# Key-value products on four column tiles, row sums of four batches in one product, and a rewritten order of steps, in a three-block transformer layer on one core

## The chip, the cores and the metric

The kernel runs on one core of one Trainium2 chip. The metric is the time of one execution on the device in microseconds (us); less is better. In the profile PE is TensorE (PEld its weight loads), DVE VectorE, ACT ScalarE, POOL GpSimd and SP SyncE, which issues most transfers.

## What is computed

The input x is 8 batches of 64 tokens with 256 features; ctx_1024 is 8 batches of 1601 rows with 256 features. Three blocks follow each other, each on a layer norm of the sum so far:

```python
x = x + xattn(layernorm(x), ctx, ctx, mask)   # 16 heads of 16, no softmax: (Q K^T / dk) V
x = x + attn(layernorm(x))                    # 16 heads, causal softmax over 64 tokens
x = x + ffn(layernorm(x))                     # rotary attention, rmsnorm, gated dense layer and 8 experts, rmsnorm
```

Since the first block has no softmax, Q (K^T V) is computed: from a batch's rows one needs the Gram matrix of ctx (256 x 256) and the sums of its rows. K^T V is kept only where row and column belong to the same head of 16 features.

## The kernel before

One program writes out the instructions of all engines. `steps_in_order` (L173) joins four tables of steps (L87 to L171), and each engine walks through the same list and issues what it has to do for a step. So the list sets the order on every engine at once; what an engine does for a step then waits on semaphores.

The 512 tokens are four tiles of 128 (two batches each), in two halves. The steps and the lines that matter here:

- `gram` n multiplies chunk n of ctx (24 chunks, three to a batch) with itself on TensorE. Before it, `split` n cuts the chunk into a high part (ScalarE) and a low part (VectorE, L1134). `evac` b copies a batch's Gram matrix out.
- `cross1` to `cross4` b make the first block of batch b. `cross1` transposes parts of the Gram matrix; `cross2_product` (L791) multiplies it with the value weights and, for odd b, multiplies the row sums of batches b-1 and b with these weights (4 products with 2 columns); `cross3` (L812) multiplies with the key weights, 4 products of 128 x 128, from which VectorE keeps the heads (L1174); `cross4` (L824) multiplies with the queries. For odd b VectorE then adds the part of the row sums (L1181) to tile b/2.
- A tile goes through `xo_product`, `turn_z`, `proj1_product`, `score_product` (L868), `turn_p`, `values`, `project` (L905), and the same again for the rotary attention (second index 1), then `square` on ScalarE, `rms1` on VectorE and GpSimd, `rms1_end` on VectorE, and `turn_x` (L938): a transpose on TensorE, a copy `xHL` on ScalarE, a subtraction on VectorE (L1261), a copy `xT` on ScalarE.
- `hidden_product`, `shared_product` and `experts_product` are the dense layers, 0 to 7 of the hidden layer for the first half, 8 to 15 for the second. They need few small steps and stand between the steps of the tiles. `hidden_product` 0 and 8 wait for the subtraction of `turn_x` of both tiles of their half.
- `norm0` i is the first layer norm of half i; on VectorE its statistics wait for the transfer of x (L1100).

All matmuls go through one helper (L698), all transposes through another (L701). A product of plain f32 operands shows as two instructions in the trace, one of the rounded type as one. The part of the code for key-value products and for the causal bars:

```python
for ob in range(KC):
    for k in range(KC):
        last = mm(ps[:, CROSS_B[0], D + ob * P:D + (ob + 1) * P], w0[:, 1, k, ob * P:(ob + 1) * P],
                  cv[:, k, ob * P:(ob + 1) * P], k == 0, k == KC - 1)
```

Of the kernel before, what the change touches and what calls it, by code (L numbers as in the profile page):

```python
# [86 lines left out]
def opening_steps():  # L87

    return [
        ("gram", 0), ("split", 0), ("gram", 1), ("split", 1), ("split", 2), ("gram", 2), ("split", 3), ("split", 4),  # L90
        ("evac", 0), ("gram", 3), ("cross1", 0), ("split", 5), ("norm0", 0), ("gram", 4), ("cross2_product", 0),
        ("gram", 5), ("norm0_end", 0), ("cross2", 0), ("split", 6), ("pre", 0), ("cross3", 0), ("evac", 1),
        ("split", 7), ("split", 8), ("q0_product", 0), ("gram", 6), ("cross4", 0), ("qb", 0), ("flag", 0),
        ("cross1", 1), ("norm0", 1), ("gram", 7), ("split", 9), ("cross2_product", 1), ("norm0_end", 1),
        ("cross2", 1), ("split", 10), ("gram", 8), ("pre", 1), ("cross3", 1), ("split", 11), ("evac", 2),
        ("q0_product", 1), ("cross4", 1), ("cross1", 2), ("gram", 9), ("qb", 1), ("flags", 0),
    ]

# [1251 lines left out]
```

## Time and profile before

| | |
|---|---|
| Median of 3 runs | 244.86 us (244.59 to 245.79) |
| The profiled execution | 244.46 us |
| Its span in the trace | 242.6 us |
| TensorE busy | 233.2 us, 96% |
| VectorE / ScalarE / GpSimd busy | 170.6 / 123.3 / 79.1 us |
| Bytes moved | 26.34 MB, 109 GB/s on average |

The span lies inside the execution's own time, 1.9 us less. The profile gives for each engine how long it was busy, for groups of instructions how long one takes, and in a timeline when each began and what ended the idle time before it. Matmuls are pipelined: the next one starts before the last one's record ends, so the distance from start to start is what one costs.

### The profile page before, as it was taken

Reading aid. Unit: us, or ns where it says so; the run is one execution under the profiler, and the core shown is the slowest. Engines: PE = TensorE matmul, PEld = TensorE weight load, DVE = VectorE, ACT = ScalarE, POOL = GpSimd, SP = SyncE. Lnnn points to the kernel's source line nnn. Section 1 sums busy time; section 2 is a strip of 40 time slices with the busy share of each in tenths; the row PEclk is TensorE's granted clock in tenths of the full one; section 3 lists DMA queues with packets and bytes.
Section 4 is the critical chain, followed back from the end, with each engine's and each line's share of the span. In section 5 each row is a group of like instructions: output and inputs, shape, how many; then the busy total and the mean of one; then the engine's idle time right before and its main releaser. Section 6 shows DMA issues by size and latency. Waiting matters only on the chain.

```text
span 242.6 us, 5335 instructions
## 1 busy us (share of the span) xinstructions
PE 233.2 (96%) x2112; PEld 210.5 (87%) x2112; DVE 170.6 (70%) x370; ACT 123.3 (51%) x246; POOL 79.1 (33%) x89
## 2 busy tenths in 40 slices
PE   6989999999999999999999999999999999999992
PEld 6979999998988989788999898997878889998881
DVE  1758885785968787978873785696999755378443
ACT  3753826266356457673455897792551444540000
POOL 3011136224423040512759359725500020650101
PEclk9999999999999999999999999999999999999998
DMA  6899999765023341803033223200000000000000
GB/s 228 270 315 387 262 400 389 280 191 170 3 86 89 97 107 69 269 5 89 0 91 93 84 86 89 86 3 0 4 0 3 0 3 0 3 22 22 5 22 22
DMA packets 9433, 26.34 MB, mean 109 GB/s; under 512 B 1464, under 2 KB 2752, under 8 KB 9280
## 3 DMA queue, kind: packets, MB, share of 16 engines
q1 hardware_dynamic: 9120, 25.47, 32.3%
q10 hardware_dynamic: 288, 0.52, 0.6%
q8 instruction: 17, 0.28, 0.5%
q14 instruction: 8, 0.07, 0.1%
HBM read 25.46 MB, written 0.52 MB: 107 GB/s over the span
## 4 chain that ended last, share of the span: by engine, by line
PE 76%; issue 6%; ACT 5%; DMA 5%; DVE 3%; POOL 2%; SPq 1%; POOLq 0%; DVEq 0%; ACTq 0%
PE ps L698 71%; PE ps L701 5%; DMA w<-in_w 3%; DMA raw<-in_ctx 2%; POOL w L495 1%; ACT probT L508 1%; ACT w L508 1%; POOL rstd L460 1%; POOL hT L499 1%; ACT L682 1%; ACT L619 1%; ACT ch L572 0%; ACT prob L619 0%; DVE Z L1292 0%; DVE cl L1134 0%
## 5 line engine op out<-in xcount | busy, mean ns | idle before, releaser
L698 PE MATMUL ps<-ch 128*128 128x130 f32 (+1 forms) x208 | 51.5, 265 | 0.9 <-DVE cl L1134 0.9
L698 PE MATMUL ps<-ch,cl 128*128 128x260 f32 (+1 forms) x208 | 51.1, 308 | 0.0
L698 PE MATMUL ps<-w,hT 128*128 128x512 f32 (+1 forms) x204 | 45.8, 382 | 0.0
L698 PEld LDWEIGHTS ps<-w,hT 128*128 128x128 f32 x204 | 36.4, 188 | 7.4 <-issue 0.3
L460 POOL TENSOR_TENSOR rstd<-ve,half_exp 128x1 f32<-128x1 f32 (+1 forms) x22 | 15.9, 723 | 82.5 <-DVE ve L1013 82.4
L1134 DVE TENSOR_TENSOR cl<-raw,ch 128x1024 fp32r<-128x1024 f32 (+4 forms) x31 | 32.7, 1069 | 11.9 <-ACT ch L572 11.6
L698 PEld LDWEIGHTS ps<-ch 128*128 128x128 f32 (+1 forms) x208 | 39.5, 190 | 1.7 <-ACT ch L572 1.0
L698 PEld LDWEIGHTS ps<-ch,cl 128*128 128x128 f32 (+1 forms) x208 | 39.2, 188 | 0.2
L572 ACT ACTIVATE ch<-raw 128x1024 fp32r<-128x1024 f32 (+4 forms) x31 | 27.7, 917 | 9.7 <-DMA raw<-in_ctx 8.6
L698 PE MATMUL ps<-xHL,dense 128*128 128x256 f32 x192 | 25.0, 287 | 0.0
L698 PEld LDWEIGHTS ps<-xHL,dense 128*128 128x128 f32 x192 | 23.6, 191 | 0.3
L495 POOL TENSOR_TENSOR w<-raw,w 128x1024 fp32r<-128x1024 f32 x8 | 18.9, 2374 | 10.1 <-ACT w L508 10.1
L1292 DVE SCALAR_TENSOR_TENSOR Z<-ps,w,Z 128x256 f32<-128x256 f32 x32 | 15.4, 482 | 7.6 <-PE ps L698 6.8
L499 POOL TENSOR_TENSOR hT<-sa,hT 128x256 fp32r<-128x256 f32 x16 | 12.7, 812 | 15.7 <-ACT hT L508 15.7
L698 PE MATMUL ps<-w,gs 128*128 128x256 f32 x64 | 15.5, 385 | 0.8 <-DMA w<-in_w 0.8
L477 POOL TENSOR_TENSOR gpre<-gab 128x130 f32<-128x130 f32 x16 | 8.4, 545 | 22.1 <-ACT gab L508 22.1
L527 ACT ACTIVATE sq<-Z 128x256 f32<-128x256 f32 x8 | 3.3, 414 | 22.8 <-DVE Z L1292 19.2
L508 ACT ACTIVATE probT<-ps 128x512 f32<-128x512 f32 x16 | 8.6, 600 | 11.0 <-PE ps L701 11.0
L698 PEld LDWEIGHTS ps<-w,gs 128*128 128x128 f32 x64 | 11.5, 189 | 2.8 <-issue 1.3
L495 POOL TENSOR_TENSOR dense<-stage,dense 128x1024 fp32r<-128x1024 f32 x4 | 9.4, 2369 | 12.6 <-ACT dense L508 12.6
L1211 DVE TENSOR_REDUCE mx<-ps 128x16 f32<-128x1024 f32 x8 | 9.8, 1221 | 4.9 <-PE ps L698 4.9
L619 ACT ACTIVATE prob<-prob 128x1024 f32<-128x1024 f32 x8 | 8.5, 1057 | 8.9 <-DVE prob L1212 8.9
(160 smaller groups left out, 429.8 us busy)
## 6 DMA issues: line engine op xcount, KB each, us to landing
raw<-in_ctx SPq DMA_DIRECT2D x22, 512.0 KB, 4.5
raw<-in_w SPq DMA_DIRECT2D x8, 512.0 KB, 3.6
stage<-in_dense SPq DMA_DIRECT2D x4, 512.0 KB, 7.2
w<-in_w SPq DMA_DIRECT2D x4, 256.0 KB, 6.1
w<-in_w SPq DMA_DIRECT2D x1, 1024.0 KB, 7.4
mask<-in_mask SPq DMA_DIRECT2D x1, 800.5 KB, 6.7
raw<-in_ctx SPq DMA_DIRECT2D x8, 65.0 KB
raw<-in_ctx ACTq DMA_DIRECT2D x2, 256.0 KB, 4.7
```

The lines of the kernel that those rows point to most:

```text
L460: pool.tensor_tensor(rstd[:, lo:hi], ve[:, lo:hi], half_exp[:, lo:hi], ALU.pow).then_inc(sem("rstd"), 1)
L477: last = pool.tensor_tensor(gpre[:, i % 2, k, :], gab[:, i % 2, k, k, :], gab[:, i % 2, k, k + 1, :], ALU.add)
L495: pool.tensor_tensor(piece(i, 1), raw_piece(i), f32(piece(i, 0)), ALU.subtract).then_inc(sem("piece_low"), 1)
L499: pool.tensor_tensor(hT[:, m // 4, 1, m % 4, :], sa[:, m % 4, :], f32(hT[:, m // 4, 0, m % 4, :]), ALU.subtract).then_inc(sem("h_low"), 1)
L508: act.activation(dst, src, ACT.Copy).then_inc(signal, 1)
L572: act.activation(halves(ch[:, c, lo:n, :])[:, :, :, 0:P], halves(raw[:, ROWS * c + lo:ROWS * c + n, :]), ACT.Copy).then_inc(sem("high_done ...
L619: act.activation(prob[:, t % 2, :, :], prob[:, t % 2, :, :], ACT.Exp, scale=SCALE).then_inc(own("prob", t), 1)
L698: return pe.matmul(o, l, r, start=start, stop=stop, skip_group_check=not check)
L701: return pe.transpose(o, src, ident)
L1134: dve.tensor_tensor(halves(cl[:, c, lo:n, :]), halves(raw[:, ROWS * c + lo:ROWS * c + n, :]), halves(f32(ch[:, c, lo:n, :]))[:, :, :, 0:P] ...
L1211: link(dve.tensor_reduce(mx[:, k, :], got, AX.X, ALU.max))
L1292: ins = dve.scalar_tensor_tensor(out=Z[:, t, :], in0=ps[:, DENSE_B[bank % 4], e * D:(e + 1) * D], scalar=w8[:, t, 2 * u + e:2 * u + e + 1] ...
```

## The change

- `cross3` on TensorE now makes only the blocks of 32 x 32 on the diagonal: for each of the 4 products of before there are 4 small ones (128 rows, 32 columns of weights, 32 moving columns), whose results stand on four different groups of 32 partitions. VectorE multiplies the smaller result, repeated, with the same mask of heads.
- Row sums: `SUMS = {1: 2, 3: 2, 7: 4}`. The sums of batches 4 to 7 go through the value weights together, in step 7. So the products of step 5 are gone, and the additions for tiles 2 and 3 come after `cross4` 7. `xo_product` 2 therefore stands behind `cross4` 7.
- Causal bars in `score_product` kind 0: the two products contract over 64 rows each instead of 128, on different halves of the rows.
- The four tables of steps are rewritten. The set of steps is the same.

```diff
+SUMS = {1: 2, 3: 2, 7: 4}
+PAIR = 2 * HD
...
-        ("gram", 0), ("split", 0), ("gram", 1), ("split", 1), ("split", 2), ("gram", 2), ("split", 3), ("split", 4),
-        ("evac", 0), ("gram", 3), ("cross1", 0), ("split", 5), ("norm0", 0), ("gram", 4), ("cross2_product", 0),
+        ("gram", 0), ("gram", 1), ("split", 0), ("split", 1), ("gram", 2), ("split", 2), ("split", 3), ("split", 4),
+        ("evac", 0), ("gram", 3), ("norm0", 0), ("split", 5), ("gram", 4), ("norm0_end", 0), ("cross1", 0),
...
-                    if i % 2:
+                    if i in SUMS:
                         pe.wait_ge(sem("scol"), i + 1)
+                        n = SUMS[i]
                         for jb in range(KC):
                             for k in range(KC):
-                                last = mm(ps[:, CROSS_B[0], jb * 2:(jb + 1) * 2], w0[:, 2, k, jb * P:(jb + 1) * P],
-                                          scol[:, k, i - 1:i + 1], k == 0, k == KC - 1)
+                                last = mm(ps[:, CROSS_B[0], jb * n:(jb + 1) * n], w0[:, 2, k, jb * P:(jb + 1) * P],
+                                          scol[:, k, i + 1 - n:i + 1], k == 0, k == KC - 1)
...
                     for ob in range(KC):
                         for k in range(KC):
-                            last = mm(ps[:, CROSS_B[0], D + ob * P:D + (ob + 1) * P], w0[:, 1, k, ob * P:(ob + 1) * P],
-                                      cv[:, k, ob * P:(ob + 1) * P], k == 0, k == KC - 1)
+                            for r in range(P // PAIR):
+                                pair = slice(ob * P + r * PAIR, ob * P + (r + 1) * PAIR)
+                                last = mm(ps[r * PAIR:(r + 1) * PAIR, CROSS_B[0], D + ob * PAIR:D + (ob + 1) * PAIR],
+                                          w0[:, 1, k, pair], cv[:, k, pair], k == 0, k == KC - 1)
...
                         for g in range(2):
-                            mm(ps[:, tile_bank(t) + g, :].rearrange("p (c k) -> p c k", k=S), unit[:, :],
-                               bars[:, :].unsqueeze(1).to_broadcast([P, H // 2, S]), True, False, False)
+                            rows_ = slice(g * S, (g + 1) * S)
+                            mm(ps[:, tile_bank(t) + g, :].rearrange("p (c k) -> p c k", k=S), unit[rows_, :],
+                               bars[rows_, :].unsqueeze(1).to_broadcast([S, H // 2, S]), True, False, False)
...
-                elif step == "cross4" and i % 2:
-                    t = i // 2
-                    dve.wait_ge(sem("qsv"), t + 1)
+                elif step == "cross4" and i in SUMS:
                     dve.wait_ge(sem("ctxT"), i + 1)
-                    mine = ctxT[:, t // TH, :, (t % TH) * P:(t % TH + 1) * P]
-                    dve.tensor_tensor(mine, mine, qbT[:, :, t * P:(t + 1) * P], ALU.add).then_inc(sem("corrected"), 1)
+                    for t in range((i + 1 - SUMS[i]) // 2, (i + 1) // 2):
+                        dve.wait_ge(sem("qsv"), t + 1)
+                        mine = ctxT[:, t // TH, :, (t % TH) * P:(t % TH + 1) * P]
+                        dve.tensor_tensor(mine, mine, qbT[:, :, t * P:(t + 1) * P], ALU.add).then_inc(sem("corrected"), 1)
```

**Opening, VectorE.** `cl` is a split's low part (128x1280 is chunk 5), `gs` are the additions of `cross1` 0, `st`, `mv` and `ve` the statistics of `norm0` 0. Before:

```order
L1134 TENSOR_TENSOR cl<-raw,ch 128x512 x4
L1142 TENSOR_TENSOR gs<-gpre,ps 128x256
L1144 TENSOR_TENSOR gs<-gab,ps 128x128
L1145 TENSOR_TENSOR gs<-gab,ps 128x128
L1134 TENSOR_TENSOR cl<-raw,ch 128x1280
L1018 BN_STATS st<-X 128x6 x2
```

With the change:

```order
L1145 TENSOR_TENSOR cl<-raw,ch 128x512 x4
L1029 BN_STATS st<-X 128x6 x2
L1032 BN_AGGR mv<-st 128x2 x2
L1024 TENSOR_SCALAR ve<-mv 128x2
L1145 TENSOR_TENSOR cl<-raw,ch 128x1280
L1040 TENSOR_SCALAR Z<-X,mv,rstd 128x256 x2
L1153 TENSOR_TENSOR gs<-gpre,ps 128x256
```

The statistics of x moved ahead of chunk 5's low part, and the additions of `cross1` 0 behind both. On TensorE `gram` 4 moved ahead of `cross1` 0, and `gram` 5 and the turn of z ahead of `cross2_product` 0.

**End of the first half's attention, TensorE.** `probT,vz` is `values` (1,1), `wo,aT` its `project`, `cv,w` `cross3`, `q0T,mb` `cross4`, `cst,Z` a turn (of z or x), `w,ctxT` `xo_product`, `xHL,dense` `hidden_product`. Before:

```order
L698 MATMUL ps<-probT,vz 32x64 x32
L698 MATMUL ps<-q0T,mb 128x64 x2
L701 MATMUL ps<-cst,gab 128x128 x4
L698 MATMUL ps<-wo,aT_99 128x256 x2
L701 MATMUL ps<-cst,Z 128x128 x2
L698 MATMUL ps<-w_52,gs 128x256 x4
L698 MATMUL ps<-scol,w_52 128x2 x4
L698 MATMUL ps<-zT,w_67 128x128 x8
L698 MATMUL ps<-cv,w_52 128x128 x4
L698 MATMUL ps<-w_67,zT 128x256 x2
L698 MATMUL ps<-q0T,mb 128x64 x2
L701 MATMUL ps<-cst,Z 128x128 x2
```

With the change:

```order
L705 MATMUL ps<-probT,vz 32x64 x32
L705 MATMUL ps<-wo,aT_99 128x256 x2
L705 MATMUL ps<-cv,w_52 32x32 x16
L708 MATMUL ps<-cst,Z 128x128 x2
L705 MATMUL ps<-q0T,mb 128x64 x2
L708 MATMUL ps<-cst,Z 128x128 x2
L705 MATMUL ps<-w_52,ctxT 128x256 x2
L705 MATMUL ps<-xHL,dense 128x256 x36
```

Behind `values` (1,1) there stood `cross4` 6 and `cross1` 7 and, behind `project` (1,1), two stages of tile 2. Now `project` (1,1) follows `values` (1,1) at once, and `cross3` 7, `cross4` 7 and two turns are all that stands between it and `xo_product` 2 and `hidden_product` 0.

**End of the second half's attention, TensorE.** `cst,prob` is `turn_p`, `w,hT` with 12 instructions is one `experts_product`. Before:

```order
L698 MATMUL ps<-w_49,hT 128x512 x36
L701 MATMUL ps<-cst,prob 128x128 x16
L698 MATMUL ps<-probT,vz 32x64 x64
L698 MATMUL ps<-wo,aT_98 128x256 x2
L698 MATMUL ps<-wo,aT_99 128x256 x2
L698 MATMUL ps<-w_49,hT 128x512 x12
L701 MATMUL ps<-cst,Z 128x128 x4
L698 MATMUL ps<-w_49,hT 128x512 x12
L698 MATMUL ps<-xHL,dense 128x256 x72
```

With the change:

```order
L705 MATMUL ps<-w_49,hT 128x512 x36
L708 MATMUL ps<-cst,prob 128x128 x16
L705 MATMUL ps<-probT,vz 32x64 x64
L705 MATMUL ps<-wo,aT_98 128x256 x2
L705 MATMUL ps<-wo,aT_99 128x256 x2
L705 MATMUL ps<-w_49,hT 128x512 x12
L708 MATMUL ps<-cst,Z 128x128 x4
L705 MATMUL ps<-xHL,dense 128x256 x96
```

One `experts_product` stood between the turns of x (`cst,Z`) and `hidden_product` 8 (`xHL,dense`); now none does.

## Rows read from the trace of the kernel before

**Rows 1.** The page, part 1: busy time, share of the span, instructions.

```profile
PE 233.2 (96%) x2112; PEld 210.5 (87%) x2112; DVE 170.6 (70%) x370; ACT 123.3 (51%) x246; POOL 79.1 (33%) x89
```

**Rows 2.** Timeline of TensorE, 14 to 19 us; in brackets the idle time before.

```profile
15.02 0.63 PE L701 MATMUL ps<-cst,gab 128*128 128x128 f32 x4 [0.44 <-ACT gab L508]
...
18.32 0.89 PE L698 MATMUL ps<-w,gs 128*128 128x256 f32 x3 [0.79 <-DMA w<-in_w]
```

**Rows 3.** Waits of TensorE: us in total, times, longest.

```profile
PE ps L698 <- ACT aT L508: 0.5, 1, 0.5
```

**Rows 4.** Groups of TensorE instructions, shapes apart: busy us, mean ns | idle before.

```profile
L698 PE MATMUL ps<-w,hT 128*128 128x512 f32 x180 | 43.0, 395 | 0.0
...
L698 PE MATMUL ps<-cv,w 128*128 128x128 f32 x64 | 8.4, 275 | 0.0
...
L698 PE MATMUL ps<-probT,vz 64*32 64x64 f32 x512 | 6.9, 224 | 0.1
...
L698 PE MATMUL ps<-q0T,mb 128*128 128x64 f32 x32 | 4.6, 268 | 0.0
...
L698 PE MATMUL ps<-blank 128*128 128x128 f32 x18 | 4.1, 423 | 1.0 <-POOL blank L443 1.0
```

**Rows 5.** Timeline of TensorE, two stretches: start us, us, instruction.

```profile
32.98 0.95 PE L698 MATMUL ps<-scol,w 128*128 128x2 f32 x8
33.79 0.31 PE L698 MATMUL ps<-ch 128*128 128x130 f32 x1
...
56.83 0.70 PE L698 MATMUL ps<-bars,unit 128*128 128x512 f32 x2
57.46 1.16 PE L698 MATMUL ps<-kblk,qp 64*128 64x128 f32 x16
```

**Rows 6.** The transfers: issue, count, size, us from issue to landing.

```profile
X<-in_x SPq DMA_DIRECT2D x1, 512.0 KB, 6.2
```

**Rows 7.** Timeline of SyncE's queue, 10 to 24 us.

```profile
11.29 0.34 SPq L407 DMA_DIRECT2D X<-in_x  x1
```

**Rows 8.** Timeline of VectorE, 10 to 24 us.

```profile
17.64 1.49 DVE L1134 TENSOR_TENSOR cl<-raw,ch 128x1280 fp32r<-128x1280 f32 x1 [0.91 <-ACT ch L572]
19.05 0.74 DVE L1018 BATCH_NORM_STATS2 st<-X 128x6 f32<-128x256 f32 x2
...
20.11 0.17 DVE L1013 TENSOR_SCALAR ve<-mv 128x2 f32<-128x2 f32 x1
```

**Rows 9.** Timeline of all engines, 110.4 to 117.9 us.

```profile
110.76 0.38 ACT L508 ACTIVATE aT<-ps 128x256 f32<-128x256 f32 x1 [1.23 <-PE ps L698]
...
112.72 0.41 DVE L1230 TENSOR_TENSOR Z<-Z,ps 128x256 f32<-128x256 f32 x1
...
113.94 0.55 POOL L460 TENSOR_TENSOR rstd<-ve,half_exp 128x1 f32<-128x1 f32 x1 [4.88 <-DVE ve L1013]
...
114.53 0.63 DVE L1041 SCALAR_TENSOR_TENSOR Z<-Z,rstd,rows 128x256 f32<-128x256 f32 x1 [0.31 <-POOL rstd L460]
```

**Rows 10.** Groups of VectorE instructions, shapes apart.

```profile
L1090 DVE CAST topf<-topi 128x16 f32<-128x16 uint32 x2 | 2.3, 1172 | 0.1
```

**Rows 11.** Timeline of all engines, 188.6 to 200 us.

```profile
197.18 0.60 PE L701 MATMUL ps<-cst,Z 128*128 128x128 f32 x4
...
197.60 0.38 ACT L508 ACTIVATE xHL<-ps 128x256 fp32r<-128x256 f32 x1 [2.02 <-PE ps L701]
...
198.54 0.39 ACT L508 ACTIVATE xT<-ps 128x256 f32<-128x256 f32 x1 [0.56 <-DVE xHL L1261]
198.82 0.38 ACT L508 ACTIVATE xHL<-ps 128x256 fp32r<-128x256 f32 x1
199.24 0.42 DVE L1261 TENSOR_TENSOR xHL<-ps,xHL 128x256 fp32r<-128x256 f32 x1 [0.73 <-ACT xHL L508]
```

**Rows 12.** Stretches: length; busy us of PE, PEld, DVE, ACT, POOL; granted clock; DMA.

```profile
237.90:240.30 2.40, 0.00 (x0) 0.00 (x0) 1.24 (x4) 0.51 (x2) 0.66 (x1) 1.00 0.00 0
240.30:242.60 2.30, 0.00 (x0) 0.00 (x0) 0.19 (x1) 0.00 (x0) 0.00 (x0) 0.51 0.17 57
```

More of the change, by code:

```diff
@@ L124, in second_half_steps @@
-        ("rotate", 1), ("keys2", 1), ("gram", 20), ("exp", (0, 1)), ("evac", 6), ("values2", 1), ("roped", 1),
-        ("keys_roped", 1), ("cross2_product", 5), ("shares", (0, 1)), ("cross2", 5), ("split", 23),
-        ("turn_p", (0, 1)), ("score_product", (1, 1)), ("values", (0, 1)), ("score", (1, 1)), ("project", (0, 1)),
-        ("square", 0), ("rms1", 0), ("exp", (1, 1)), ("cross3", 5), ("rms1_end", 0), ("gram", 21), ("cross4", 5),
-        ("cross1", 6), ("piece", 3), ("turn_x", 0), ("piece", 4), ("shares", (1, 1)), ("gram", 22),
@@ L129, in second_half_steps @@
-        ("cross2_product", 6), ("xo_product", 2), ("cross2", 6), ("xo", 2), ("xo_end", 2), ("norm1", 2), ("gram", 23),
-        ("turn_p", (1, 1)), ("cross3", 6), ("evac", 7), ("values", (1, 1)), ("cross4", 6), ("norm1_end", 2),
-        ("cross1", 7), ("piece", 5), ("piece", 6), ("project", (1, 1)), ("turn_z", (2, 0)), ("cross2_product", 7),
-        ("cross2", 7), ("square", 1), ("proj1_product", 2), ("rms1", 1), ("cross3", 7), ("queries", 2), ("keys1", 2),
-        ("rms1_end", 1), ("values1", 2), ("cross4", 7), ("turn_x", 1), ("piece", 7), ("score_product", (2, 0)),
@@ new lines, in second_half_steps @@
+        ("score", (1, 0)), ("cross4", 4), ("cross1", 5), ("exp", (1, 0)), ("norm2_end", 0), ("shares", (1, 0)),
+        ("split", 21), ("gram", 18), ("split", 22), ("gram", 19), ("turn_z", (0, 1)), ("cross2_product", 5),
+        ("proj2_product", 0), ("cross2", 5), ("turn_p", (1, 0)), ("keys2", 0), ("rotate", 0), ("values", (1, 0)),
+        ("roped", 0), ("cross3", 5), ("keys_roped", 0), ("project", (1, 0)), ("values2", 0), ("gram", 20),
+        ("score_product", (0, 1)), ("norm2", 1), ("piece", 2), ("norm2_end", 1), ("evac", 6), ("turn_z", (1, 1)),
@@ new lines, in second_half_steps @@
+        ("turn_p", (1, 1)), ("square", 0), ("cross2_product", 7), ("rms1", 0), ("rms1_end", 0), ("piece", 6),
+        ("cross2", 7), ("values", (1, 1)), ("project", (1, 1)), ("cross3", 7), ("square", 1), ("rms1", 1),
+        ("turn_x", 0), ("rms1_end", 1), ("cross4", 7), ("turn_x", 1), ("xo_product", 2), ("hidden_product", 0),
+        ("hidden_product", 1), ("xo", 2), ("xo_end", 2), ("norm1", 2), ("norm1_end", 2), ("hidden", 0),
+        ("hidden_product", 2), ("xo_product", 3), ("turn_z", (2, 0)), ("xo", 3), ("hidden", 1), ("piece", 7),
@@ L153, in second_half_steps @@
-        ("experts_product", (1, 3)), ("last_square", 0),
+        ("project", (2, 1)), ("project", (3, 1)), ("square", 2), ("square", 3), ("rms1", 3), ("rms1", 2),
+        ("rms1_end", 3), ("rms1_end", 2), ("experts_product", (1, 3)), ("turn_x", 3), ("turn_x", 2),
     ]
```

133 lines of the change are left out of this document (72 added, 61 removed), and 3 rows, old and new, of the table USES.

## The prediction

> **What bounds the kernel now.** I read the page's first part, then TensorE's groups, then its waits, then the timeline at the places where the order changes. The page says that TensorE is busy 233.2 of 242.6 us, and no other engine over 171 [rows 1]. TensorE's waits are few: the reader is to see that the two largest of the opening lie in its timeline, 0.44 us before `cross1` 0 and 0.79 us before `cross2_product` 0 [rows 2], and that the list has one of 0.5 us for ACT's copy `aT`, between a `values` and its `project` [rows 3]. So between the first products and the last, work taken from TensorE comes off the time, and each new wait of TensorE goes on top. The other engines matter only where TensorE runs out of other work while they hand over a tile.
>
> **What is taken from TensorE.**
>
> *Key-value products.* One batch's `cross3` has 8 instructions with full weights: 8.4 us over 8 batches, 1.05 each [rows 4]. Now it has 32, each on a quarter of the columns. The nearest row is `values`, which also alternates among four column groups: 512 instructions in 8 blocks take 6.9 us, 0.86 a block of 64 [rows 4]. Both figures hold some 0.2 us in which only the last instruction drains. Half a block costs 0.33 + 0.2 = 0.53, which would save 0.52. But `values` also uses two row groups, which the new products can't. I take 0.60, a saving of 0.45, and 3.6 us over 8 batches. One end: the groups hide nothing of each other, the instructions cost a quarter of a full one's (1.05 - 0.2) / 8 = 0.106, 32 x 0.027 = 0.85, and nothing is saved. Other end: the rate of `values` and a little more, 0.55 saved, 4.4 us.
>
> A rule speaks against the small products. The Trainium skill ("TensorE: Matmul & The Clock Gate", section "Wait — 56ns, not 53.3ns?") says that matmuls never start less than about 25 ns apart, however small. By it 32 would take an estimated 0.8 us, the saving would be 0.05 to 0.1 a batch, and the time about 3 us above my sum. The trace disagrees for tiles: 64 instructions of `values` in 0.86 us are 13 ns apart with the drain counted in [rows 4].
>
> *Row sums.* A step's 8 instructions take from 32.98 to 33.79, 0.81 us, though they have two columns [rows 5]. With four columns I take the same. One step of four goes: 0.8 us. GpSimd and VectorE do the same multiplications and additions, only later.
>
> *Bars.* Two instructions from 56.83 to 57.46, 0.63 us [rows 5]. On two halves of the rows they can run together, as the pairs after them do: 16 instructions of `kblk,qp` in 1.16 us. I take half, 0.31 saved, 1.25 over four tiles; ends 0 and 1.25.
>
> Together 3.6 + 0.8 + 1.25 = 5.65 us, with ends 0.8 and 6.45. VectorE's multiplication with the heads has as many elements as before and costs nothing new.
>
> **What the order adds.**
>
> *Opening.* x is issued at 11.29 and lands 6.2 us later, at 17.5 [rows 6, 7]. Before, chunk 5's low part came first (17.64, 1.49 us), and the statistics after it, by which time x was there [rows 8]. Now VectorE stands at the statistics until 17.5, needs from 19.05 to 20.28, 1.23 us, for them, and ends chunk 5 at 17.5 + 1.25 + 1.5 = 20.25. `gram` 5 can't start before about 20.3. TensorE has less to do till then: `gram` 4 took from 15.46 (15.02 and 0.44 for four transposes, 0.63 less the drain) to the wait before 18.32, which began at 17.53 [rows 2], less the drain 1.9 us. It can now follow `gram` 3 at about 14.5, ends at 16.4, `cross1` 0 at 16.8. So TensorE idles 3.5 us, where it lost 0.44 + 0.79 and about 0.3 of restarting. The loss is 2.0 us. `cross2_product` 0 waits for the additions behind chunk 5 and fills nothing. SyncE's queue, which loads chunk 8 when chunk 5's low part is done, is later by the same microsecond, and has three chunks in hand. Nothing later gives this back, since TensorE hardly waits there. Ends: 1.0, if x lands a microsecond earlier, and 2.5.
>
> *Before `xo_product` 2.* `project` (1,1) now directly follows `values` (1,1): that is the 0.5 us of [rows 3], at 110.76 in [rows 9]. From a `project` to the turn of its x: hand-over 0.2, then from the addition at 112.72 to the end of the scaled row at 114.53 + 0.63 = 115.16 [rows 9]; 2.7 us with the hand-over to TensorE. The cover is `cross3` 7 (0.5), a turn of two transposes (0.22) and `cross4` 7 (4.6 us over 8 batches is 0.57 [rows 4]), some 1.25. 1.5 us stay open. `xo_product` 2 waits then for the additions that ACT's `ctxT` and VectorE make behind that chain, an estimated 0.4. In all 2.4 us. Queued behind VectorE's wait for the mean square are the remainder of `turn_x` 0 and these additions. GpSimd's root has `piece` 6 and two multiplications with the row sums ahead of it, which could add up to 0.5. Ends 0.5 and 3.0.
>
> *Second half, rotary part.* `project` (2,0) on VectorE stands behind `shares` (3,0) and `gate_best` 0, a string of small instructions, of which one conversion alone takes 1.17 us [rows 10]. TensorE has `values` (3,0) and one `experts_product` as cover, 0.86 + 12 x 0.24 = 3.7 us [rows 4], against 2.7 for the chain and the queue ahead. I take 1.0 us; ends 0 and 2.
>
> *Before `hidden_product` 8.* The reader is to see in [rows 11] that four transposes start at 197.18, and that the second tile's `xHL` is subtracted until 199.66; one `experts_product` covered it. Now `experts_product` (1,3) stands ahead of the turns, where it covers the roots, and nothing follows them. From 197.2 to 199.7 less 0.44 of transposes is 2.1 us of idle TensorE. Ends 1.5 and 2.5.
>
> What I cost at nothing: the rest of the first half, where `gram` chunks stand in twos and threes and tiles 0 and 1 move against them, a few tenths of waits for a few tenths; the tail, where `finish` 2 moved behind the last experts' additions, beside ACT's square (that cover is 0.6 us, about its size); the bars' copies on ACT.
>
> **Sum.** 244.46 - 5.65 + 2.0 + 2.4 + 1.0 + 2.1 = 246.3 us. It is made against the profiled execution, which lies 0.4 under the median of 244.86. A measurement of this kernel tells 0.5% (1.2 us) from no change, so the forecast is just over that line.
>
> **The rivals.**
>
> 1. *The hand-overs are covered, and it is faster.* The two places that I had to piece together from several engines' queues, before `xo_product` 2 and in the rotary part, cost nothing, and the products save their upper end: 244.46 - 0.8 - 1.25 - 4.4 + 2.0 + 2.1 = 242.1. It decides once these two places together stay below about 1 us. For it: in the old order TensorE waits at almost none of its hand-overs. Against it: the covers counted above are short. Chance 0.27.
> 2. *Savings and waits cancel.* Half of those two places: 244.6. Chance 0.15.
> 3. *The clock falls in the opening.* After its last matmul TensorE stood still from 237.9, and the granted clock was 1.00 until 240.3 and 0.51 after it [rows 12]: it fell from 2.4 to 1.2 GHz after 2.4 us of standing. The opening's new gap is 3.5 us. The start shows the price of a stretch at the lower level: its 18 instructions took 4.1 us [rows 4], 0.22 each, where four transposes of the same size take 0.60 with the drain [rows 11], 0.11 each; that loses some 2 us, so 248.2. For it: the gap is longer than that at the end; against it: matmuls surround it. Chance 0.12.
> 4. *The column groups don't run side by side*, so the change doesn't do what it says: 246.3 + 3.6 = 249.9. `values` speaks against it. The Trainium skill (same page, section "LDWEIGHTS (loading the stationary operand)") says that a weight load's time goes with its columns alone; if loads don't overlap, that is this rival. Chance 0.10.
>
> **The numbers.** My own case has 0.36, of which 0.10 falls short of the line. Slower: 0.26 + 0.12 + 0.10 = 0.48; within 0.5%: 0.15 + 0.10 = 0.25; faster: 0.27. The range is 241.7 to 248.6: it takes in the first three rivals and leaves out the fourth, 0.10, and the far ends of the first and third, 0.1 together.
>
> **What would show it.** `cv,w` as 256 instructions with 4.5 to 5 us busy instead of 8.4; `scol,w` x24; bars at 0.3 us a pair. A wait of TensorE of 3 us or more before `gram` 5 near 17 us, ended by VectorE's `cl`, at clock 1.00. Waits of 1 to 2 us before the turn of x 1, and 2 us before `hidden_product` 8, ended by `xHL`. TensorE busy around 228 us. I am wrong if `cv,w` stays near 8 us, or if `gram` 5 starts by 19, or if no wait shows between `project` (1,1) and `hidden_product` 0.

## The result, and the profile after

| | before | after |
|---|---|---|
| Median | 244.73 us (244.45 to 245.79, 4 runs) | 249.69 us (248.79 to 250.67, 4 runs) |
| Ratio | | 1.0196, 95% interval 1.0164 to 1.0228 |
| The profiled execution | 244.46 us | 248.79 us |
| Its span, mean granted clock | 242.6 us, 0.995 | 247.0 us, 0.981 |

The kernel became 5.0 us slower. I had forecast 246.3 and a range up to 248.6: the direction was right, the size was not, and the time lies outside the range. The ratios here and below leave out executions more than 1.5% above the fastest of their kernel, which are two of e1's (248.92 and 249.55 us); medians and ranges have all of them.

The page of the changed kernel, part 1, answers to [rows 1]:

```profile
PE 232.2 (94%) x2296; PEld 206.8 (84%) x2296; DVE 172.6 (70%) x368; ACT 119.4 (48%) x243; POOL 81.0 (33%) x89
```

TensorE is busy almost as long as before, though it has less to do. Its groups, shapes apart (busy us, mean ns | idle before), answer to [rows 4]:

```profile
L705 PE MATMUL ps<-cv,w 128*32 128x32 f32 x256 | 3.7, 199 | 1.9 <-DVE svn L1178 1.9
...
L705 PE MATMUL ps<-bars,unit 64*128 64x512 f32 x8 | 2.0, 494 | 0.0
...
L705 PE MATMUL ps<-scol,w 128*128 128x2 f32 x16 | 1.9, 241 | 0.0
...
L705 PE MATMUL ps<-scol,w 128*128 128x4 f32 x8 | 1.0, 242 | 0.0
```

Key-value products take 3.7 us instead of 8.4, and one step of row sums is gone. Something else has grown. TensorE's waits (us in total, times, longest) answer to [rows 3]:

```profile
PE ps L705 <- DVE cl L1145: 4.2, 3, 3.0
PE ps L705 <- DVE svn L1178: 1.9, 1, 1.9
PE ps L705 <- DVE xHL L1276: 1.7, 1, 1.7
PE ps L705 <- POOL blank L447: 1.0, 1, 1.0
PE ps L705 <- ACT aT L512: 0.5, 1, 0.5
```

The first is the opening, the third stands before `hidden_product` 8, and both were forecast. The second, for the value sums `svn` ahead of `cross3` 7, was not. The stretches around it (length; busy us of PE, PEld, DVE, ACT, POOL; granted clock; DMA), first of the kernel before, then of the changed one:

```profile
124.00:128.55 4.55, 4.55 (x90) 3.96 (x90) 2.85 (x9) 4.03 (x9) 2.34 (x4) 1.00 0.29 104
128.55:135.40 6.85, 6.85 (x52) 6.10 (x52) 2.67 (x9) 3.23 (x11) 4.76 (x4) 1.00 0.53 150
```

```profile
0.00:22.00 22.00, 16.82 (x118) 15.94 (x119) 10.57 (x21) 9.93 (x18) 4.94 (x16) 1.00 0.85 282
22.00:124.00 102.00, 101.66 (x1169) 92.41 (x1171) 79.91 (x147) 60.09 (x109) 37.01 (x33) 1.00 0.49 165
124.00:128.55 4.55, 2.16 (x80) 1.54 (x68) 4.05 (x7) 0.72 (x3) 3.02 (x4) 1.00 0.63 169
128.55:135.40 6.85, 6.61 (x24) 5.29 (x24) 4.13 (x13) 3.16 (x8) 1.81 (x3) 0.50 0.11 44
135.40:197.00 61.60, 61.48 (x632) 53.03 (x633) 47.85 (x103) 32.20 (x72) 24.88 (x21) 1.00 0.09 27
```

The reader is to see the fourth line of the second block: busy 6.61 of 6.85 us, and only 24 matmuls done, at a granted clock of 0.50. TensorE ran at 1.2 GHz there instead of 2.4. A busy engine looks healthy; the count and the clock column tell that it is not.

What started it is in the timeline of all engines (start us, us, instruction, idle time before):

```profile
124.06 2.34 POOL L499 TENSOR_TENSOR w<-raw,w 128x1024 fp32r<-128x1024 f32 x1
124.11 2.56 DVE L1052 SCALAR_TENSOR_TENSOR Z<-Z,rstd,rows 128x256 f32<-128x256 f32 x1 [1.43 <-POOL rstd L464]
...
126.71 0.87 DVE L1167 SCALAR_TENSOR_TENSOR cv<-rows,gpre,ps 128x256 f32<-128x256 f32 x2
127.50 0.35 DVE L1178 TENSOR_SCALAR svn<-ps,bvn 128x4 f32<-128x4 f32 x2
...
128.00 0.46 PE L705 MATMUL ps<-cv,w 128*32 128x32 f32 x32 [1.91 <-DVE svn L1178]
...
128.38 0.57 PE L708 MATMUL ps<-cst,Z 128*128 128x128 f32 x2
```

VectorE's scaled row of tile 0 takes 2.56 us instead of some 0.5. GpSimd's subtraction of `piece` 6 had begun 0.05 us before it; when that ends, at 126.40, the row goes through. `cv` and `svn` stand behind it on VectorE, and `cross3` 7 waits for them.

The kernel before had such a pair in its own trace, the other way round, VectorE's low part of a chunk first and GpSimd's root (0.55 to 0.73 us in most places) held by it:

```profile
77.22 1.49 DVE L1134 TENSOR_TENSOR cl<-raw,ch 128x1280 fp32r<-128x1280 f32 x1
...
77.38 1.75 POOL L460 TENSOR_TENSOR rstd<-ve,half_exp 128x1 f32<-128x1 f32 x1 [3.77 <-DVE ve L1013]
```

**The sum by stages.** The table is worked out from the starts of all matmuls. Each shape gets the distance to the next start that it has where nothing waits (a `cross3` block 0.81 before and 0.39 after, a pair of bars 0.62 and 0.32); what is beyond that is idle time, drains at hand-overs and a low clock together. The cuts stand at the same times, not at the same work, so a few tenths may lie in the neighbouring row. e1 is the first experiment below.

| us | before | after | e1 |
|---|---|---|---|
| Price of all matmuls | 212.0 | 206.7 | 206.7 |
| Beyond it, to 22 us | 7.0 | 9.2 | 8.7 |
| 22 to 124 | 13.4 | 12.3 | 12.4 |
| 124 to 135.4 | 0.8 | 6.6 | 2.9 |
| 135.4 to 197 | 3.4 | 3.7 | 4.0 |
| 197 to the end | 0.0 | 2.6 | 2.2 |
| Last matmul starts | 237.5 | 241.9 | 237.7 |

### The profile page after: what moved, and what is told of

The parts are those of the page before. It is cut to its first block, busy times and chain, and to the rows that moved or that the text cites. A ratio compares the mean times of both kernels' runs of the same rounds, so it can differ in the third digit from the quotient of the medians.

```text
span 247.0 us, 5698 instructions
## 1 busy us (share of the span) xinstructions
PE 232.2 (94%) x2296; PEld 206.8 (84%) x2296; DVE 172.6 (70%) x368; ACT 119.4 (48%) x243; POOL 81.0 (33%) x89
## 4 chain that ended last, share of the span: by engine, by line
PE 79%; DMA 5%; issue 4%; DVE 4%; ACT 3%; POOL 2%; SPq 1%; POOLq 0%; DVEq 0%
PE ps L705 74%; PE ps L708 5%; DMA X<-in_x 3%; DMA raw<-in_ctx 2%; DVE Z L1052 1%; DVE cl L1145 1%; POOL w L499 1%; ACT probT L512 1%; POOL gpre L481 1%; DVE xHL L1276 1%; POOL rstd L464 0%; ACT xHL L512 0%; ACT ch L579 0%; ACT w L512 0%; DVE Z L1307 0%
## 5 line engine op out<-in xcount | busy, mean ns | idle before, releaser
L1145 DVE TENSOR_TENSOR cl<-raw,ch 128x1024 fp32r<-128x1024 f32 (+4 forms) x31 | 31.9, 1049 | 9.9 <-ACT ch L579 9.6
L705 PE MATMUL ps<-xHL,dense 128*128 128x256 f32 x192 | 25.8, 295 | 1.7 <-DVE xHL L1276 1.7
L705 PEld LDWEIGHTS ps<-xHL,dense 128*128 128x128 f32 x192 | 24.7, 200 | 2.1 <-DVE xHL L1276 2.0
L499 POOL TENSOR_TENSOR w<-raw,w 128x1024 fp32r<-128x1024 f32 x8 | 19.7, 2461 | 3.9 <-ACT w L512 3.9
L503 POOL TENSOR_TENSOR hT<-sa,hT 128x256 fp32r<-128x256 f32 x16 | 11.5, 738 | 17.0 <-ACT hT L512 17.0
L499 POOL TENSOR_TENSOR dense<-stage,dense 128x1024 fp32r<-128x1024 f32 x4 | 10.9, 2729 | 10.1 <-ACT dense L512 10.1
L1291 DVE TENSOR_TENSOR sa<-sa,ps 128x256 f32<-128x256 f32 x16 | 6.6, 418 | 7.6 <-ACT sa L689 7.5
```

Of the source, the lines that this page charges most:

```text
L499: pool.tensor_tensor(piece(i, 1), raw_piece(i), f32(piece(i, 0)), ALU.subtract).then_inc(sem("piece_low"), 1)
L503: pool.tensor_tensor(hT[:, m // 4, 1, m % 4, :], sa[:, m % 4, :], f32(hT[:, m // 4, 0, m % 4, :]), ALU.subtract).then_inc(sem("h_low"), 1)
L705: return pe.matmul(o, l, r, start=start, stop=stop, skip_group_check=not check)
L1145: dve.tensor_tensor(halves(cl[:, c, lo:n, :]), halves(raw[:, ROWS * c + lo:ROWS * c + n, :]), halves(f32(ch[:, c, lo:n, :]))[:, :, :, 0:P] ...
L1291: dve.tensor_tensor(sa[:, m % 4, :], sa[:, m % 4, :], ps[:, DENSE_B[use % 4], TOK:2 * TOK], ALU.mult).then_inc(sem("taken"), 1)
```

## The experiments

Two things had to be told apart at 124 us: whether the block of VectorE by `piece` 6 alone sets off wait and clock, and what else the new order costs. One kernel stands in each heading; all but e5 and e6 start from the changed kernel. The kernel before ran beside each: 244.5, 244.6 and 244.75 us in the three series (e1 to e4 on one chip, e5 to e8 and e9 to e12 on another); the changed kernel wasn't repeated with them, its times are those of the result. Each kernel has one profiled execution; of the others only time and mean clock are known. A fall of the clock for 3.4 us takes 0.007 off the mean of some 243 us, the low clock behind the last matmul up to 0.006, so a mean of 0.994 or more is an execution without a fall on the way, called "with the clock up" below.

**e1: `piece` 6 later.**

```diff
-("rms1_end", 0), ("piece", 6), ("cross2", 7),
+("rms1_end", 0), ("cross2", 7),
...
-("cross4", 7), ("turn_x", 1),
+("cross4", 7), ("piece", 6), ("turn_x", 1),
```

> The changed kernel, but piece 6 (a copy on ScalarE, a subtraction of 2.34 us on GpSimd) stands behind cross4 7 instead of ahead of cross2 7. Theory A: the 1.9 us wait of TensorE before cross3 7 comes from VectorE's scaled row of tile 0 at 124.11, which took 2.57 us instead of 0.49 because GpSimd's subtraction of piece 6 had started 0.05 us before it; and this wait makes the granted clock fall at 128.55 for 6.85 us. Then the row takes 0.5 us, the wait before cross3 7 shrinks to 0.3 us or less, the clock stays at 1.00 there, and the time falls by 2.0 + 3.4, to about 244. Theory B: the wait is that of the order itself (project (1,1) directly behind values (1,1), little cover before cross3 7). Then the wait stays over 1 us, the clock falls all the same, and the time stays within 1 us of 249.7.

Measured: 246.24 us (244.61 to 249.55, 8 runs), ratio 1.0056 [1.0028, 1.0084]; 3.5 us less than the changed kernel. Its timeline of all engines, and below it the two stretches:

```profile
123.67 0.49 DVE L1053 SCALAR_TENSOR_TENSOR Z<-Z,rstd,rows 128x256 f32<-128x256 f32 x1 [1.43 <-POOL rstd L465]
...
125.57 0.46 PE L706 MATMUL ps<-cv,w 128*32 128x32 f32 x32
...
128.03 0.44 PE L709 MATMUL ps<-cst,Z 128*128 128x128 f32 x2 [0.79 <-DVE Z L1053]
```

```profile
124.00:128.55 4.55, 3.05 (x47) 1.98 (x45) 3.71 (x12) 2.31 (x7) 1.74 (x3) 1.00 0.41 119
128.55:135.40 6.85, 6.78 (x48) 6.19 (x49) 4.83 (x14) 3.38 (x8) 3.62 (x3) 1.00 0.26 77
```

The row takes 0.49 us, `cross3` 7 doesn't wait, and in the profiled execution (244.61) the clock stays at 1.00 through the stretch, in which 48 matmuls run instead of 24. But the executions differ: three of 244.6 to 245.3 at mean clock 0.996, two of 246.2 at 0.989, three of 247.2 to 249.6 at 0.974 to 0.981. The clock can still fall, only not every time. The wait is as theory A had it, and so are clock and time (about 244) of the profiled execution, but not the median.

**e2: the wait stays, TensorE is given work.**

```diff
 elif step == "cross3":
+    if i == B - 1:
+        for _ in range(8):
+            mm(ps[:, GRAM_B[0], 0:P], ident, ident, True, True)
     pe.wait_ge(sem("cv"), i + 1)
```

> The changed kernel with 8 products of the identity with itself (16 instructions, 1.75 us) into a free PSUM bank, issued just ahead of cross3 7, where TensorE waits 1.9 us. They fill the wait and do nothing else. Theory A, clock: the low clock from 128.55 to 135.4 costs about 3.4 us by itself. Then the clock stays at 1.00 there, and the time falls by 2.5 to 3.4 us though the wait stays as long. Theory B: the clock falls for another reason, or the work in that stretch is bound by ScalarE and VectorE and not by TensorE's rate, so that the time stays within 0.7 us.

Measured: 248.01 us (246.16 to 249.16, 4 runs), ratio 1.0158 [1.0131, 1.0185]. The profiled execution took 246.16 at mean clock 0.996:

```profile
125.44 1.95 PE L706 MATMUL ps<-cst 128*128 128x128 f32 x16
127.52 0.46 PE L706 MATMUL ps<-cv,w 128*32 128x32 f32 x32
```

Each of the 8 products is two instructions in the trace, so they take 1.9 us and just fill the wait. `cross3` 7 starts 2 us later than in e1, as in the changed kernel (where all of this part lies 0.5 later), but the clock doesn't fall: 2.6 us less than the changed kernel's 248.79. `xo_product` 3, the first step behind the low clock, starts as follows in the changed kernel, in e2 and in e1:

```profile
138.28 1.02 PE L705 MATMUL ps<-w,ctxT 128*128 128x256 f32 x4
...
135.65 1.02 PE L706 MATMUL ps<-w,ctxT 128*128 128x256 f32 x4
...
134.10 1.02 PE L706 MATMUL ps<-w,ctxT 128*128 128x256 f32 x4
```

At `project` (1,1), ahead of the wait, the three start at 124.95, 124.48 and 124.51, so the changed kernel had lost 0.5 us before. What is left is 2.2 us between it and e2, the clock, and 1.6 us between e2 and e1, the blocked row. These are two costs, as theory A had it, the clock's below its 2.5 to 3.4. The low clock cost 2.2 and not half of its 6.83 us, since TensorE stood behind other engines for a part of it: 0.9 us of it were lost when `hidden_product` 0 starts (132.51 against 131.16), the rest after that. That the filling keeps the clock up rests on more than one profile: the executions of the changed kernel, e3 and e4, which have the wait unfilled, all twelve lie at 0.976 to 0.986, and three of e2's four at 0.990 or above. The medians of e2 and the changed kernel are 1.7 us apart. The other three executions of e2, at 0.993, 0.990 and 0.981, were not profiled; two of them at least have a fall somewhere.

**e3: the opening in the order of before.** The first 28 steps stand in the order of before, as far as the later ones allow.

```diff
-("gram", 0), ("gram", 1), ("split", 0), ("split", 1), ("gram", 2), ("split", 2), ("split", 3), ("split", 4),
-("evac", 0), ("gram", 3), ("norm0", 0), ("split", 5), ("gram", 4), ("norm0_end", 0), ("cross1", 0),
+("gram", 0), ("split", 0), ("gram", 1), ("split", 1), ("split", 2), ("gram", 2), ("split", 3), ("split", 4),
+("evac", 0), ("gram", 3), ("cross1", 0), ("split", 5), ("norm0", 0), ("gram", 4), ("cross2_product", 0),
...
```

> The changed kernel with the opening order of the kernel before up to the flag step (chunk 5 before the statistics of x on VectorE, cross1 0 and cross2_product 0 ahead of gram 4 and gram 5 on TensorE). Theory A: the opening costs 2.0 us net, as the sum had it (TensorE stands 3.0 us before gram 5 at 20.57). Then the wait before gram 5 is below 0.3 us and the time falls by 1.7 to 2.2 us. Theory B: the microseconds are given back later (the transfers or splits bound the first 60 us), so that the time falls by less than 0.7 us.

Measured: 249.2 us (248.99 to 250.52, 4 runs), ratio 1.0205 [1.0172, 1.0238]: no gain. The 3.0 us before `gram` 5 are gone, and others have come:

```profile
45.59 1.99 PE L706 MATMUL ps<-w,gs 128*128 128x256 f32 x8 [0.69 <-DVE gs L1157]
...
51.70 0.46 PE L706 MATMUL ps<-cv,w 128*32 128x32 f32 x32 [0.88 <-DVE cv L1168]
```

By the method of the table, 7.0 us are lost to 22 us, as before, and 12.1 to 52, against 12.0 in the changed kernel. What TensorE saves at the start it waits out by 52 us: theory B.

**e4: `experts_product` around the last turns as before.**

```diff
-("experts_product", (1, 2)), ("shares", (2, 1)),
+("shares", (2, 1)),
...
-("project", (3, 1)), ("square", 2), ("square", 3), ("rms1", 3), ("rms1", 2),
-("rms1_end", 3), ("rms1_end", 2), ("experts_product", (1, 3)), ("turn_x", 3), ("turn_x", 2),
+("project", (3, 1)), ("experts_product", (1, 2)), ("square", 2), ("square", 3), ("rms1", 3), ("rms1", 2),
+("rms1_end", 3), ("rms1_end", 2), ("turn_x", 3), ("turn_x", 2), ("experts_product", (1, 3)),
```

> The changed kernel with experts_product (1,2) moved behind the two projects of the second half and experts_product (1,3) behind the turns of x 3 and 2, as in the kernel before. Theory A: the 1.7 us wait before hidden_product 8 goes and nothing takes its place, since turn_p had slack: 1.5 to 2 us less. Theory B: the third and fourth tile are themselves the chain (they begin later), so that the wait moves to turn_p (2,1) or (3,1), where experts_product (1,2) was the cover: the time stays within 0.5 us.

Measured: 248.78 us (248.03 to 250.21, 4 runs), ratio 1.0187 [1.0145, 1.0228], 0.9 less, in a range that overlaps the changed kernel's (248.79 to 250.67). Of the profiled executions, 0.2 apart, e4 gains 0.5 us from `xo_product` 3 to the end. The wait for `xHL` is gone, and one has come between `turn_p` (2,1) and `turn_p` (3,1):

```profile
191.52 1.04 PE L709 MATMUL ps<-cst,prob 128*128 128x128 f32 x8
193.94 1.09 PE L709 MATMUL ps<-cst,prob 128*128 128x128 f32 x8 [1.38 <-DVE prob L1237]
```

So the wait moved, as theory B has it, but to the second of the two.

**e5: the kernel before with the column groups alone.** Its order, row sums and bars are those of before; VectorE's multiplication with the heads is changed along with the products.

```diff
-last = mm(ps[:, CROSS_B[0], D + ob * P:D + (ob + 1) * P], w0[:, 1, k, ob * P:(ob + 1) * P],
-          cv[:, k, ob * P:(ob + 1) * P], k == 0, k == KC - 1)
+for r in range(P // PAIR):
+    pair = slice(ob * P + r * PAIR, ob * P + (r + 1) * PAIR)
+    last = mm(ps[r * PAIR:(r + 1) * PAIR, CROSS_B[0], D + ob * PAIR:D + (ob + 1) * PAIR],
+              w0[:, 1, k, pair], cv[:, k, pair], k == 0, k == KC - 1)
```

> The kernel before, its order and its row sums untouched, with the key-value products on four column groups alone. Theory A: TensorE bounds the kernel and the new products cost 0.46 us a batch (3.7 us busy over 8 batches in the changed kernel) instead of 1.05, so that the time falls by 3 to 4.7 us, to about 240.5. Theory B: the gain is eaten where TensorE arrives earlier than the other engines or the transfers, and the time falls by less than 1.5 us.

Measured: 243.43 us (242.88 to 243.77, 6 runs), ratio 0.9949 [0.993, 0.9969]. The products take 3.7 us instead of 8.4, and the kernel gains 1.2: theory B. Waits that the kernel before has less of or not at all:

```profile
PE ps L703 <- ACT gab L510: 1.0, 2, 0.5
...
PE ps L700 <- ACT z0T L510: 0.5, 2, 0.3
```

From a block's start to the next instruction's start is 7.1 us over the 8 blocks before, 4.7 here, and 3.4 in the changed kernel. In the old order what follows a block isn't ready: `z0T` after the first two, for example.

**e6: column groups and bars in the order of before.** e5, ScalarE's copy `unit` laid out for two halves of the rows, and:

```diff
-mm(ps[:, tile_bank(t) + g, :].rearrange("p (c k) -> p c k", k=S), unit[:, :],
-   bars[:, :].unsqueeze(1).to_broadcast([P, H // 2, S]), True, False, False)
+rows_ = slice(g * S, (g + 1) * S)
+mm(ps[:, tile_bank(t) + g, :].rearrange("p (c k) -> p c k", k=S), unit[rows_, :],
+   bars[rows_, :].unsqueeze(1).to_broadcast([S, H // 2, S]), True, False, False)
```

> The kernel before with the column groups and with the bars on two halves of the rows, order and row sums untouched. Theory A: another 0.8 us less than the kernel with the columns alone (2.8 us of busy time before, 2.0 in the changed kernel), about 239.8, so that the parts without the order beat both kernels. Theory B: no difference to the columns alone.

Measured: 242.59 us (242.3 to 243.78, 6 runs), ratio 0.9929 [0.9905, 0.9952]. This beats both kernels: 2.0 us under the one before. It is 0.8 under e5, as much as theory A gave the bars, though the ranges of the two overlap; the 239.8 of theory A was built on a gain that e5 didn't have.

**e7: e1, and the statistics of x behind chunk 5.**

```diff
-("gram", 3), ("norm0", 0), ("split", 5), ("gram", 4),
+("gram", 3), ("split", 5), ("norm0", 0), ("gram", 4),
```

> The changed kernel with piece 6 later, and with the statistics of x behind chunk 5's low part, everything else in the opening as the change has it. Theory A: the wait before gram 5 (2.7 us in the kernel with piece 6 later) comes from VectorE standing at the statistics until x lands: it shrinks to 1.5 us or less, the clock no longer falls in some executions, the executions agree within 1 us, and the median falls from 246.2 to 244.5 or less. Theory B: the median stays within 0.7 us of 246.2, because the low part of chunk 5 isn't what the next 20 us wait for, and the executions spread as before.

Measured: 245.98 us (244.49 to 246.34, 4 runs), ratio 1.0061 [1.0037, 1.0084]. The wait before `gram` 5 falls from 2.7 us in e1 to 0.9, and `gram` 5 starts 1.4 us earlier (18.57 against 20.02). With the clock up the time is e1's (244.49 and 244.61), and the median is within 0.3 of e1's, which is theory B. But none of the four executions lies at 0.974 to 0.981, as three of e1's did: one at 0.997, three at 0.988 to 0.990.

**e8: e1, and TensorE given work in the opening.**

```diff
+if i == 5:
+    for _ in range(12):
+        mm(ps[:, CHAIN_B + 1, 0:P], ident, ident, True, True)
```

> The changed kernel with piece 6 later and 12 products of the identity with itself (24 instructions, 2.6 us) into a free bank just ahead of gram 5, where TensorE waits 2.7 to 3.0 us. Theory A: the spread of the executions with piece 6 later (244.6 to 249.5, mean clock 0.997 to 0.974) is the clock falling in the opening's wait in some executions. Filled, all executions lie within 1.5 us of each other at a mean clock over 0.99, with a median of about 245. Theory B: the spread has another cause and stays.

Measured: 246.04 us (244.45 to 247.8, 10 runs), ratio 1.0055 [1.0022, 1.0088]. Five executions of 244.45 to 245.25 at 0.995 to 0.997, five of 246.8 to 247.8 at 0.988 to 0.990. One of the latter was profiled:

```profile
124.00:129.74 5.74, 4.24 (x111) 3.02 (x111) 4.29 (x12) 2.58 (x8) 2.29 (x5) 1.00 0.33 96
129.74:133.16 3.42, 3.42 (x14) 3.12 (x13) 2.00 (x6) 2.01 (x4) 2.86 (x2) 0.50 0.00 0
```

Here the clock fell behind the hand-overs before `xo_product` 2, where no single wait of TensorE is over 0.8 us. The fall isn't all that sets this execution, of 246.83, 2.2 us behind e1's profiled one: 1.0 us of it was there by 33 us, its matmuls run at half the pace until 10.3 us where e1's do until 5.7, and 1.2 came with the fall. Theory A fails: with the opening's gap filled, two groups some 2 us apart remain. Executions as low as e1's slowest three don't come in e7 and e8, which shorten or fill that gap, but whether e1's had a fall in the opening is not shown: none of the three was profiled, e7 and e8 ran on another chip, and no trace of this case has a fall there.

**e9: the new order with the operations of before.** e7's order, and the diffs of e5, e6 and e10 taken back to what the kernel before has.

```diff
-SUMS = {1: 2, 3: 2, 7: 4}
+SUMS = {1: 2, 3: 2, 5: 2, 7: 2}
...
-for r in range(P // PAIR):
...
-rows_ = slice(g * S, (g + 1) * S)
```

> The order of e7 (the changed order, with piece 6 behind cross4 7 and the statistics of tile 0 behind chunk 5's low part) with the operations of the kernel before: 8 key-value products with full weights, row sums in pairs, bars over all 128 rows. e7 took 245.98 in the median, 244.49 with the clock up. Theory A (the three parts are worth in this order what the prediction gave them, 3.6 + 0.8 + 1.25 = 5.65 us): 251.6, and 250.1 with the clock up. Theory B (they are worth little in any order, as in e5, where 4.7 us less of busy TensorE gave 1.2): about 248. What this run has over the kernel before is the price of the new order alone.

Measured: 249.65 us (248.77 to 251.34, 5 runs), ratio 1.021 [1.0175, 1.0245]. This lies between the theories: against e7, the three parts are worth 3.7 us in the median and 4.3 between the fastest executions. Against e10, which differs by columns and bars alone, these two are worth 4.1 us in this order (3.7 between the fastest); in the old one, e6 against before, 2.0. The order itself costs 4.9 us, even with both repairs in it. In the profiled execution the clock fell at a third place, behind the wait for `xHL`:

```profile
202.00:205.75 3.75, 2.03 (x16) 1.56 (x15) 2.37 (x6) 2.38 (x5) 0.00 (x0) 1.00 0.00 0
205.75:209.16 3.41, 3.41 (x19) 3.41 (x18) 1.92 (x5) 0.97 (x3) 0.00 (x0) 0.50 0.00 0
```

**e10: e7 with the row sums in pairs.**

```diff
-SUMS = {1: 2, 3: 2, 7: 4}
+SUMS = {1: 2, 3: 2, 5: 2, 7: 2}
```

> e7 with the row sums in pairs again (steps 1, 3, 5 and 7, two columns each), everything else as in e7. Theory A (a step of 8 instructions costs its 0.8 us wherever it stands): 0.8 over e7, 246.8, and 245.3 with the clock up. Theory B (it stands where TensorE waits anyway, or it gives svn earlier to cross3 7 and costs less): within 0.2 of e7.

Measured: 245.55 us (245.03 to 246.49, 8 runs), ratio 1.0032 [1.0016, 1.0049]. Neither theory held in the median, which is 0.4 under e7's. The step costs 0.81 us again at 90.72, and the fastest run is 0.5 slower than e7's; but seven of eight executions have the clock at 0.995 or above, where e7 had one of four. So the four columns may lose in how often the clock falls what they save; with four executions of e7 this isn't settled.

**e11: e7, and TensorE given work before two turns.**

```diff
 elif step == "turn_x":
+    if i < 2:
+        for _ in range(4):
+            mm(ps[:, CHAIN_B + 3, 0:P], ident, ident, True, True)
```

> e7 with 4 products of the identity with itself, 0.11 us each, ahead of each of the turns of x of tiles 0 and 1, where TensorE's timeline has gaps; they go to a bank that nobody reads then and change no result. e7's and e8's executions lie in two groups, at mean clock 0.995 to 0.997 and at 0.988 to 0.990, some 2 us apart. Theory A (the slower group is the clock that falls for 3.4 us in the stretch before xo_product 2, and it stays up if TensorE has something to do there): no execution below 0.993, and all near 244.8 (244.49 and up to 0.4 for products that do not fit in their gap). Theory B (the clock's fall has another place or reason): two groups as before, median 246.

Measured: 245.75 us (244.94 to 247.73, 11 runs), ratio 1.0053 [1.0031, 1.0075]. Eight of eleven executions lie at 0.994 or above, between 244.94 and 246.02, where e7 had one of four and e8, whose turns aren't filled either, five of ten; two remain at 0.988. This points to theory A but doesn't show it: theory A wanted no execution below 0.993, the counts are small, and e10 has seven of eight without any filling. In the profiled executions the filled kernel loses 0.9 us against e7 in this stretch, so the filling isn't free, and the median gains 0.2.

**e12: e7, e4's edit, and shares (2,1) ahead of scores (3,1).**

```diff
-("exp", (2, 1)), ("experts_product", (1, 1)), ("score", (3, 1)),
-("experts_product", (1, 2)), ("shares", (2, 1)),
+("exp", (2, 1)), ("experts_product", (1, 1)), ("shares", (2, 1)), ("score", (3, 1)),
```

> e7 with e4's edit (experts_product (1,2) behind project (3,1), experts_product (1,3) behind the turn of x of tile 2) and the weights' shares of (2,1) ahead of the scores' addition of (3,1) on VectorE. e4 took away the 1.7 us before hidden_product 8 and got 1.4 before turn_p (2,1). Theory A (that 1.4 was the shares standing behind the other tile's scores on VectorE): the wait before turn_p falls to under 0.6, and the run lies 1.0 to 1.6 under e7 at the same clock, 243.2 with the clock up. Theory B (the wait is the chain scores, exponential, shares itself): 1.2 or more stays there or before turn_p (3,1), and the time is that of e7.

Measured: 246.38 us (245.11 to 246.75, 7 runs), ratio 1.0076 [1.0062, 1.009]. The wait before `turn_p` grew:

```profile
PE ps L709 <- DVE prob L1237: 2.5, 1, 2.5
```

Theory A falls: the scores of tile 3, now behind VectorE's wait for tile 2's exponential, are late instead, and the 2.5 us stand between the two `turn_p`. That is where e4's wait stood too, so the expectation had put it at the wrong tile, and the edit delayed the tile that was already late. As in e4, moving the cover moved the hole.

## Why the prediction was wrong

**Savings: right on TensorE, too much in time.** 3.6 + 0.8 + 1.25 = 5.65 forecast. Start to start, the 8 blocks of `cross3` went from 7.1 to 3.4 us, the 4 steps of row sums from 3.24 to 2.50 for 3, the 4 pairs of bars from 2.54 to 1.33: 5.6. I had chosen 0.60 a block; it is 0.39 with a quick successor. The rule of the Trainium skill ("TensorE: Matmul & The Clock Gate", section "Wait — 56ns, not 53.3ns?"), that matmuls start no closer than about 25 ns, doesn't fit this trace for tiles: from 128.00 to 128.38 there are 32, 12 ns each with the hand-over to the next step counted in. In measured time e9 against e10 gives 4.1 us for columns and bars, of 4.85 forecast, and e9 against e7 gives 3.7 to 4.3 for all three parts, of 5.65. Rival 4 is out. What I had left out is that these savings depend on the order: in the old one columns and bars are worth 2.0 (e6), since the next instruction isn't ready.

**Opening: right in size, wrong about what follows.** 2.0 forecast, 2.2 by the table; `gram` 5 starts at 20.57 (forecast 20.3) after 3.00 us. But I wrote that nothing later gives this back. 1.1 us come back between 22 and 124, and e3 shows that without the gap TensorE meets others by 52 us. e7 against e1, both with the clock up, puts the price of most of this gap at 0.1 us. Rival 3, a fall of the clock here, is seen in no trace: the falls profiled in the changed kernel, e3, e4 and e8 begin at 128.6 to 129.9 us, e9's at 205.8. Its price, read from the kernel's first matmuls, rests on their halved pace alone; the clock column has 1.00 from 1.00 to 4.80 us.

**Before `xo_product` 2: this is the step that failed.** The term was 2.4 us, of 0.5 for `aT`, 1.5 for the hand-over and 0.4 for the additions, with 3.0 as its upper end. It measured 5.8. Without `piece` 6 in the way (e1) the stretch loses 2.1 more than before, of waits of 0.5, 0.2 and 0.8 and the drains beside them, so the term as I had made it was right. Two things were missing from it, 3.7 us together:
- *`piece` 6 against VectorE, 1.6 us.* I counted `piece` 6 only as something queued ahead of a root on GpSimd, worth up to 0.5. It was over at 126.40, before that root, tile 1's, was due (129.09). What mattered was that both engines had an instruction reading SBUF at the same time. The row takes 2.56 us where GpSimd began first and 0.49 where it didn't (e1). The Trainium skill ("SBUF — State Buffer", section "Who interferes with whom") says that a VectorE operation with two SBUF inputs and a GpSimd operation that reads SBUF exclude each other for a whole instruction, whoever starts first; the trace agrees, with 2.56 against 0.49. TensorE waited 1.9 us for it, of which 1.6 are left at `xo_product` 3 (e2 against e1). I didn't ask which pairs the new order puts side by side.
- *The clock, 2.2 us.* From 124.00 to 128.55 TensorE was busy for 2.16 us. Then it ran at 1.2 GHz for 6.83 us, which cost 2.2 (the changed kernel against e2). In my term the clock stood at nothing, without a reason. This is rival 3's mechanism, but I looked for it in the opening alone, at the one gap that was longest. It fell at a stretch of several short gaps. That rival 3's 248.2 comes near the measured time is chance: it has the loss at another place.

**Rotary part: too much.** 1.0 forecast, 0.3 by the table for all of 135.4 to 197, with no wait in the list. The cover of `values` and `experts_product` was enough, the lower end.

**Before `hidden_product` 8: right.** 2.1 forecast, a wait of 1.73, 2.6 with the drains around it. e4 shows that putting the cover back gains 0.5 us of it between the profiled executions, as a wait of 1.4 comes before `turn_p` (3,1); e12's order on VectorE makes that wait longer, 2.5, and whether another order would remove it stays open.

Put together by the table: 244.46 - 5.3 + 2.2 - 1.1 + 5.8 + 0.3 + 2.6 = 249.0, against 248.79 profiled. With 2.1 in place of 5.8 it is 245.3; e1 with the clock up took 244.6 to 245.3. So without the missing 3.7 us the forecast of 246.3 would have been 1.0 too high: opening and rotary part cost 0.9 and 0.7 less than forecast, `hidden_product` 8 0.5 more. (In the median e1 took 246.24, with the clock falling in some executions.) The other two rivals, a faster kernel and a cancelling one, fell with the measured waits. What stays open is what decides, in one and the same kernel, whether the clock falls in an execution.

## What to carry to other kernels

When an order changes, list for every long GpSimd instruction what VectorE runs beside it, not only what is queued behind it: two engines that each have time can still stop each other (2.56 us for a row of 0.49). Price a place where several short waits meet by what the clock may do, not only by the waits, and look at the count of instructions in a stretch, since a slow clock shows as busy time. A saving on the bounding engine is worth its full price only where the next instruction is ready; test it alone in the old order before the order is rewritten around it.
